# Query projections by halves of the sequence, the second half among the scores, and the first layer norm one sequence sooner

## What is computed

```python
x = x + _layernorm(attn(_layernorm(x)))     # below
x = x + _layernorm(ffn(_layernorm(x)))      # 8 experts, top 2, silu(x Wg) * (x Wu), Wd

q = relu(split(h @ Wq, 16)); k = relu(split(h @ Wk, 4)); v = split(h @ Wv, 4)
gk = log_sigmoid(split(h @ Wg1 @ Wg2 + bg2, 4)) / 16
# per head of 64: S_t = exp(g_t) * S_{t-1} + k_t (outer) v_t ; o_t = (q_t / 8) @ S_t
o = g_norm_weight * (o * rsqrt(mean(o * o) + 1e-6))
attn = o.reshape(b, t, 1024) @ Wo
```

## Time and profile before

| | |
|---|---|
| three runs | 1250.46, 1253.17, 1254.14 us; median 1253.17 |
| profiled execution | 1251.32 us, of which the span of the instructions is 1249.5 us |
| mean granted TensorE clock | 0.978 of full speed |
| busy in the span | PE 93%, DVE 62%, ACT 51%, POOL 44% |
| busy in 50 us of the first stage (265 to 315) | PE 47.3, DVE 38.7, ACT 28.6, POOL 27.3 us |
| chain that ended last | PE 69%, DVE 15%, issue 7%, ACT 4%, DMA 3% |

### The profile page before, as it was taken

The page is one execution under the profiler, slowest core; times in us unless marked ns, Lnnn a source line. Parts: engine busy times, 40 slices in busy tenths (PEclk is TensorE's granted clock), DMA queues, the critical chain, the costliest instruction groups (busy, mean ns, idle before and its releaser), DMA issues.

```text
span 1249.5 us, 29218 instructions
## 1 busy us (share of the span) xinstructions
PE 1158.4 (93%) x8910; PEld 942.3 (75%) x8910; DVE 769.4 (62%) x2380; ACT 640.8 (51%) x1653; POOL 556.0 (44%) x686
## 2 busy tenths in 40 slices
PE   8999999999999999999999999579999999999895
PEld 4867867768668678677686686569999989998762
DVE  5677777777777777777777876723333333333327
ACT  3655656547546556465475473334444444443336
POOL 2245464564654654645646544423333333333326
PEclk9999999999999999999999999879999999999998
DMA  7001010010110110100101101334111111111534
GB/s 277 10 27 31 13 43 19 24 34 17 34 34 11 40 32 11 42 17 25 39 12 34 34 4 35 139 89 133 47 49 49 47 49 46 49 49 44 177 124 176
DMA packets 59676, 67.50 MB, mean 54 GB/s; under 512 B 6896, under 2 KB 49664, under 8 KB 59264
## 3 DMA queue, kind: packets, MB, share of 16 engines
q1 hardware_dynamic: 48720, 41.10, 10.5%
q0 software_dynamic: 8448, 17.45, 4.2%
q10 hardware_dynamic: 2480, 8.61, 2.1%
HBM read 37.98 MB, written 29.15 MB: 54 GB/s over the span
## 4 chain that ended last, share of the span: by engine, by line
PE 69%; DVE 15%; issue 7%; ACT 4%; DMA 3%; DVEq 1%; POOL 1%; ACTq 0%; SPq 0%; POOLq 0%
PE pO L764 9%; PE pO L597 9%; PE pO L602 7%; PE pA L581 6%; PE pW L630 5%; PE pA L755 4%; PE pA L756 4%; PE pJ L755 4%; PE pJ L756 4%; PE pT L613 3%; DVE S_raw L1130 2%; DVE qT L1116 2%; PE pJ L630 2%; PE pJ L515 2%; DVE ss L1160 2%
## 5 line engine op out<-in xcount | busy, mean ns | idle before, releaser
L1630 POOL DMA_INDIRECT expert_out<-y,tail x136 | 130.5, 960 | 262.0 <-ACT y L1023 238.5
L874 ACT ACTIVATE sq<-pO 128x512 f32<-128x512 f32 x128 | 75.9, 593 | 211.7 <-PE pO L597 160.5
L597 PE MATMUL pO<-vJ,aT 128*128 128x128 f32 x1024 | 144.5, 285 | 14.4 <-DVE aT L1153 14.4
L597 PEld LDWEIGHTS pO<-vJ,aT 128*128 128x128 f32 x1024 | 128.7, 196 | 37.0 <-issue 34.1
L1542 POOL DMA_INDIRECT expert_rows<-x1n,rowi x120 | 120.5, 1004 | 50.0 <-issue 31.7
L1160 DVE TENSOR_REDUCE ss<-sq 128x8 f32<-128x512 f32 x128 | 87.1, 680 | 80.1 <-ACT sq L874 78.4
L764 PE MATMUL pO<-wdown_sb,vJ 128*128 128x128 f32 x1088 | 133.3, 276 | 0.0
L764 PEld LDWEIGHTS pO<-wdown_sb,vJ 128*128 128x128 f32 x1088 | 127.4, 193 | 0.0
L1408 DVE TENSOR_TENSOR vJ<-pA,kJ 128x256 f32<-128x256 f32 x136 | 57.5, 425 | 107.8 <-ACT kJ L1012 107.2
L602 PE MATMUL pO<-S_mid,qT 128*128 128x128 f32 x896 | 118.3, 275 | 0.0
L602 PEld LDWEIGHTS pO<-S_mid,qT 128*128 128x128 f32 x896 | 109.0, 192 | 0.0
(11 more groups left out here) (234 smaller groups left out, 2374.0 us busy)
## 6 DMA issues: line engine op xcount, KB each, us to landing
xt<-expert_rows SPq DMA_DIRECT2D x69, 130.0 KB
xa<-x SPq DMA_DIRECT2D x16, 256.0 KB, 2.8
xr<-x SPq DMA_DIRECT2D x16, 256.0 KB
after_attention<-x SPq DMA_DIRECT2D x16, 256.0 KB
arena<-after_attention ACTq DMA_DIRECT2D x8, 512.0 KB
expert_rows<-zeros SPq DMA_DIRECT2D x8, 390.0 KB
expert_out<-y,tail POOLq DMA_INDIRECT x136
wgate_sb<-wgate SPq DMA_DIRECT2D x1, 2048.0 KB, 9.4
```

Source lines behind the costliest of these rows:

```text
L597: last = mm(o[:, g, h, :, :], aT[:, c % 2, h, g * P:(g + 1) * P], vJ[:, c, h, :], start=(h == 0 and g == 0), stop=(c == 0), skip_group_che ...
L1630: g.indirect_dma_start(out=ys_dram, in_=y[:, k, :], in_offset=None, out_offset=bass.IndirectOffsetOnAxis(ap=tail[:, k, 1:2].bitcast(U32), ...
```

## The change

The eight query products are made for the first 256 tokens at the end of a turn as before, two products of 256 columns in one bank, and for the last 256 tokens as four pairs inside `chunks`: one before the first scores, one after them, one behind the second scores and one behind `outputs(i, 1)`. `scores(i, 0)` waits for the first four reads, `scores(i, 4)` for all eight. `query` on DVE reads a pair, and its last four are in `chunks`. In a bank the two products are interleaved in blocks of 64 columns (n r c), so that DVE reads and writes runs of 128; `grow` is kept twice over (ACT writes 1024 columns per pair instead of 512), in the place of the two gate buffers behind the others, and `on` moves to another place of the same arena.

The norm of sequence i + 2 begins in turn i: statistics at chunk 3 on DVE, rstd at chunk 3 on ACT, `norm_apply` on POOL between the first gate sum and the first gate difference. Router statistics move from chunk 0 to 1, `router_rstd` from 1 to 2 (ahead of `norm_T`), router transposes from 2 to 3. The last tile's `merged_apply` moves behind the first two masks, its residual on POOL behind `mids`. The query decays of pair 1 are made right after its key decays. The loops of ACT, DVE and POOL leave one turn more outside, for the last one has no norm ahead.

```diff
-            def project_queries(j, turns=range(PAIRS * R)):
-                for b in turns:
-                    if b < 2:
-                        pe.wait_ge(v_ready, j * 8 + 4 * b + 4)
-                    elif b < 4:
-                        pe.wait_ge(k_ready, j * 2 + b - 1)
+            def project_queries(j, half, turns=range(PAIRS * R // 2)):
+                for n in turns:
+                    if half == 0 and n < 2:
+                        pe.wait_ge(v_ready, j * 8 + 4 * n + 4)
+                    elif half == 0:
+                        pe.wait_ge(k_ready, j * 2 + n - 1)
                     else:
-                        pe.wait_ge(q_ready, j * 8 + b - 3)
-                    mm(four[b % 4][:], wq_sb[:, b // R, b % R, :], xnT[:],
-                       start=True, stop=True).then_inc(q_psum, 1)
+                        pe.wait_ge(q_ready, j * 8 + n + 3)
+                    for u in range(2):
+                        b = 2 * n + u
+                        last = mm(query_bank(n, half).rearrange("p (n r c) -> p r n c", r=2, c=C)[:, u, :, :], wq_sb[:, b // R, b % R, :],
+                                  xnT[:, half * (L // 2):(half + 1) * (L // 2)], start=True, stop=True)
+                    last.then_inc(q_psum, 1)
...
                 if c >= 2:
                     pe.wait_ge(a_ready, i * NC + c)
-                else:
+                if c == 0:
+                    pe.wait_ge(q_ready, i * 8 + 4)
+                elif c == 4:
                     pe.wait_ge(q_ready, i * 8 + 8)
...
+                project_queries(i, 1, range(0, 1))
                 scores(i, 0)
+                project_queries(i, 1, range(1, 2))
                 for c in range(NC):
                     outputs(i, c)
+                    if c == 1:
+                        project_queries(i, 1, range(3, 4))
                     if more and c == 2:
                         norm_transposes(i + 1, routed)
                     if c % 2 == 0 and c + 2 < NC:
                         scores(i, c + 2)
+                    if c == 0:
+                        project_queries(i, 1, range(2, 3))
                     if c in (3, 5, 7):
                         merge_heads(i, (c - 3) // 2, more)
                     if c > 0:
                         out_transposes(i, c - 1)
+                    if routed and c == (3 if more else 2):
+                        router_transposes(i - 1, i - 1, x1n)
                     if more and c in (2, 3):
                         gate_logits(i + 1, c - 2)
-                    if routed and c == 2:
-                        router_transposes(i - 1, i - 1, x1n)
...
             def query_decays(j, p):
-                a(grow[:, p, :], rel[:, p, :], ACT.Exp, scale=-1.0 / GATE_NORMALIZER).then_inc(decay_ready, 1)
+                a(grow[:, p, :, :, :], wide(rel[:, p, :].rearrange("p (n c) -> p n c", c=C).unsqueeze(2), P, NC, 2, C),
+                  ACT.Exp, scale=-1.0 / GATE_NORMALIZER).then_inc(decay_ready, 1)
...
-                    if more and c == 0:
+                    if more and at_start(i) and c == 0:
                         norm_rstd(i + 1)
-                    if routed and c == 1:
+                    if ahead and c == 3:
+                        norm_rstd(i + 2)
+                    if routed and c == (2 if more else 1):
                         router_rstd(i - 1, i - 1)
                     if more and c == 2:
                         norm_T(i + 1)
...
                     if more and c == 7:
-                        key_decays(i + 1, 1)
+                        decays(i + 1, 1)
...
-            def query(j, b):
+            def query(j, n, half):
                 dve.wait_ge(decay_ready, j * 4 + 4)
-                dve.wait_ge(q_psum, j * 8 + b + 1)
+                dve.wait_ge(q_psum, j * 8 + 4 * half + n + 1)
...
                     state(j, 0)
                     state(j, 1)
-                    merged_apply(merging, NT - 1)
-                for b in range(PAIRS * R):
-                    query(j, b)
...
+                    query(j, 0, 0)
+                    state(j, 2)
+                    query(j, 1, 0)
+                    query(j, 2, 0)
+                    state(j, 3)
+                    query(j, 3, 0)
...
+                for c in range(4, NC - 1):
+                    state(j, c)
...
                 mask(i, 0)
                 mask(i, 1)
-                if more:
+                if routed:
+                    merged_apply(i - 1, NT - 1)
+                query(i, 0, 1)
+                query(i, 1, 1)
+                if more and at_start(i):
                     norm_stats(i + 1)
                 for c in range(NC):
+                    if ahead and c == 3:
+                        norm_stats(i + 2)
                     head_norm(i, c, not more)
-                    if routed and c == 0:
+                    if c < 2:
+                        query(i, 2 + c, 1)
+                    if routed and c == (1 if more else 0):
                         router_stats(i - 1)
...
-                    if c == 1 and merging is not None:
-                        residual(merging, NT - 1)
...
-            def turn(i, routed, more):
-                if more:
+            def turn(i, routed, more, ahead):
+                if routed:
+                    residual(i - 1, NT - 1)
+                else:
                     norm_apply(i + 1)
...
                     gate_sum(i + 1, 0)
+                if ahead:
+                    norm_apply(i + 2)
+                if more:
                     gate_relative(i + 1, 0)
```

More of the change, by code:

```diff
@@ L128, in gate_view @@
             return flat[:, n * PAIRS * L:(n + 1) * PAIRS * L].rearrange("p (a l) -> p a l", a=PAIRS)
-        absz, relz, run, rel, grow, shrink = (gate_view(n) for n in range(6))
+        absz, relz, run, rel, shrink = (gate_view(n) for n in range(5))
+        grow = flat[:, 6 * PAIRS * L:8 * PAIRS * L].rearrange("p (a n r c) -> p a n r c", a=PAIRS, r=2, c=C)
         step_log = sb("step_log", [P, PAIRS, NC])
@@ L228, in build, with query_bank @@
         merge_bank = [pW[:, 0:HID], pJ[0][:, 0:HID], pW[:, 0:HID], pW[:, 0:HID]]
+        def query_bank(n, half):
+            return four[n][:] if half == 0 else four[2 + n % 2][:]
         def gate_bank(j, p):
@@ L700, in _ @@
             pe.wait_ge(q_in, 16)
-            project_queries(0, range(0, 1))
+            project_queries(0, 0, range(0, 1))
             key_transposes(0)
-            project_queries(0, range(1, 2))
+            project_queries(0, 0, range(1, 2))
             state_updates(0)
-            project_queries(0, range(2, PAIRS * R))
+            project_queries(0, 0, range(2, 4))
             pe.wait_ge(rest_in, 16 * len(REST_W))
@@ L716, in turn @@
                 state_updates(i + 1)
[L717 removed]
+                project_queries(i + 1, 0)
             turn(0, False)
@@ L932, in chunks @@
                     if more and c == 7:
-                        query_decays(i + 1, 1)
                         steps_of(i + 1)
@@ L974, in _, with turn @@
             act.wait_ge(rest_in, 16 * len(REST_W))
-            def turn(i, routed):
-                chunks(i, True, routed)
+            def turn(i, routed, ahead=True):
+                chunks(i, True, routed, ahead)
                 out_T(i, NC - 1)
@@ L982, in _ @@
             turn(0, False)
-            with act.Fori(1, S - 1) as i:
+            with act.Fori(1, S - 2) as i:
                 act.preload_act_table_set(LOG_EXP)
@@ L986, in _ @@
             act.preload_act_table_set(LOG_EXP)
-            chunks(S - 1, False, True)
+            turn(S - 2, True, False)
+            chunks(S - 1, False, True, False)
             router_T(S - 1, HALVES[0])
@@ L1139, in queries_and_states @@
                     state(j, 1)
-                    merged_apply(merging, NT - 1)
-                for b in range(PAIRS * R):
-                    query(j, b)
[L1143 to L1148, removed]
+                    query(j, 0, 0)
[5 more added lines that the diff above has]
+                else:
+                    for n in range(4):
+                        query(j, n, 0)
+                        state(j, n)
+                for c in range(4, NC - 1):
+                    state(j, c)
             def mask(i, c):
@@ L1360, in _ @@
             turn(0, False)
-            with dve.Fori(1, S - 1) as i:
+            with dve.Fori(1, S - 2) as i:
                 turn(i, True)
-            chunks(S - 1, False, True)
+            turn(S - 2, True, False)
+            chunks(S - 1, False, True, False)
             choose(S - 1, S - 1, HALVES[0])
@@ L1491, in router_norm, with mids @@
                                     ALU.subtract, ALU.mult).then_inc(x1n_ready, 1)
-            def mids(j, merging=None, after={}):
+            def mids(j, after={}):
                 pool.wait_ge(step_ready, j + 1)
@@ L1600, in turn, with turn_and_mids @@
                         scatter(1, n)
-            turn(0, False, True)
-            mids(1, 0)
```

(13 more changed lines are left out.)

14 lines of the change are left out of this document (9 added, 5 removed).

## The result

The changed kernel takes 1236.9 us (median of four runs, 1234.9 to 1240.0), the kernel before 1253.7 in the same comparison: a ratio of 0.987, 95% interval 0.985 to 0.989. Of the forecast's 21.5 us, 16.8 came, and 1236.9 lies just inside the upper end of the forecast of 1224 to 1237. The profiled execution took 1237.6 us, of which the span is 1234.5.

The account below looks back on a forecast made before the run. PE, busy 93% of the span, bounds the kernel, so only its waits or slow running can be won. Turns 9.8, turn 0 1.4, last turn 2.3 and clock 8.0 make 21.5 us: 1231 forecast, range 1224 to 1237 (wider 1214 to 1244).

Parts of the forecast that it names:

- the walk: One turn followed step by step on PE, DVE and ACT with durations from the profile: turn 0.70 us shorter.
- the pair of gaps: PE's waits before a turn's first scores and first outputs, 2.28 us; three short waits, 0.66 in all, should replace them.
- rival (2): DVE's stretch denser than counted: waits of 0.5 more a turn stay, or clock still falls; 1238 to 1246, chance 0.20.
- The gate logits' wait: New PE wait in chunk 2 for xnT, behind the router's statistics and rstd: 0.91 us lost per turn.
- the sum: Turns 1 to 14 9.8 us, turn 0 1.4, last turn 2.3, clock 8.0; together 21.5.
- Rival (1): The wait at the gate logits is hidden: 12.7 us more, 1218; chance 0.17.
- The clock: Five turns' falls of the granted clock behind the pair of gaps vanish, 1.6 us each, 8.0 in all.
- Turn 0: First turn, without router: scores start at 29.2 instead of 30.34 with two pairs still to come; gain 1.4 us.
- The last turn: No norm_T there: first half gives 1.6 us, PE's 0.81 wait for router rows mostly goes; gain 2.3.
- The other edits: Decays, norm a sequence sooner and moved residual lie under cover; norm_apply 3.13 us on POOL, from 335.2 to 338.3.
- rival (4): Query products slowed by writes in blocks of 64 columns; at twice their 0.86 us the kernel takes 1340; chance 0.03.
- rival (5): Late load of xa stops DVE in chunk 3, slower from 1.5 us a turn; with late decays, chance 0.07.

Follow-up runs that it names:

- the shifted kernel: The changed kernel with three empty instructions more on ACT and three on DVE ahead of their first turns; 1229.67 us, ratio 0.981 to before.

## Why the prediction was right, and where it was off

**The bound and the walk held.** Scores and sixth pair came within 0.01 us of the walk. Where signals are on time (the shifted kernel, its turn moved by 41.62 us) `outputs` came at 360.69 where the walk had 360.72, the router's statistics at 368.88 (walk 368.91), and `outputs(4)` at 377.64 (walk 377.80). The three short waits at the start of a turn replaced the pair of gaps. One remark made under rival (2) did not hold, that DVE has under 0.9 us free in this stretch: in the shifted kernel it stands idle 1.23 us in one wait alone. That costs nothing here, and it is why the statistics of the norm fit in at their old place.

**The gate logits' wait was mis-sized.** The step has 0.91 us per turn; in the run with `norm_T` first it proved to be 0.69, and 0.10 for the slower products behind it, so 0.79. The statistics stood where the walk had them, but from their start to that of the logits it took 2.50 us (373.42 to 375.92), not 2.71: two short instructions on ACT took 0.44 instead of 0.56, the copy 0.58 instead of 0.62, and PE followed 0.05 behind it, not 0.13. Without the late signals the turn is 0.88 shorter than 48.46, where the sum has 0.70. Rival (1), that the wait is hidden, did not happen. Where the signals are on time the whole gain is 23.2 us by the medians (1252.83 to 1229.67), against the sum's 21.5.

**The late signal stood in no step.** The walk lets DVE's mask start when DVE is free, at 364.01 by this turn's clock, and it started at 364.41. Of the 0.88 a turn this took back 0.43, in 13 turns 5.6 us: 12.7 for the turns 1 to 14 became 7.0, and the sum had 9.8. It is rival (2) in its price (waits of 0.5 a turn that stay) but not in its reason: DVE was not denser than counted, it stood still.

**The clock** was sized rightly inside the turns. All five falls in the turns are gone, at 1.57 us each 7.9 of the 8.0 counted, and the kernel before with filled gaps shows it by itself. The single wait at the gate logits led to none; but it is 0.53 us long and not the 0.91 of the forecast, so that no run here tests a single gap of that size. Slices below full clock remain at the start, which the second profiled execution of this kernel doesn't have, and from 782.6 to 786.0 us, in the hand-over to the experts, where the kernel before is still at full clock. The last tile's product by Wo, in before and then in after:

```profile
796.94 2.05 PE L630 MATMUL pW<-wo_sb,oT 128*128 128x128 f32 x16
```

```profile
782.39 3.63 PE L639 MATMUL pW<-wo_sb,oT 128*128 128x128 f32 x16
```

This fall costs 1.5 us, and no step of the forecast has it. Six of the eleven profiled executions with the split queries have it, so it doesn't come with the change as such; why some have it stays open.

**Turn 0 was over-valued**: 1.4 in the sum, 0.6 between the marks. The walk of a later turn was applied to it, but in turn 0 `queries_and_states` has another order: behind the last read four states come, not three, and the last of them starts only after DVE has stood idle 0.56 us for the one before it. The mask follows at 31.54, so PE's wait for it stayed as long as in a turn of before. DVE and then PE in turn 0 after:

```profile
31.15 0.47 DVE L1151 SCALAR_TENSOR_TENSOR S_raw<-S_raw,step,pO 128x64 f32<-128x64 f32 x2 [0.56 <-DVE S_raw L1151]
...
32.28 1.16 PE L606 MATMUL pO<-vJ,aT 128*128 128x128 f32 x8 [0.94 <-DVE aT L1177]
```

**The last turn** gave a little less than was counted. The sum has 2.3, and 1.6 for the fifth fall, 3.9 together. The last tile's product by Wo starts 44.70 us behind the last mark before and 41.34 after, so 3.4 came, and 3.7 where the signals are on time. The 0.81 that PE waited for router rows is gone. That 3.8 came in all behind the last mark is luck of this execution: the fall in the hand-over took 1.5 back, and the experts and the final norm, which the change doesn't touch, happened to take 2.0 less. They differ by 2.7 us between the two profiled executions of the kernel with ACT's and DVE's programs moved.

**The other edits** cost PE nothing. The blocks of 64: rival (4) fell, and with it, for this pattern, the rule of the Trainium skill that it rests on. The decays with 1024 columns took 1.04 us each, between the bounds of 0.6 and 1.2. `xa` landed in 3.0 us (2.8 before), and DVE waits for it once, 4.2 us at the start (4.5 before), and never in the turns, so rival (5) fell. `norm_apply` took 4.09 us where 3.13 was counted, from 381.24 to 385.33; that is 1 us of the cover of 1.6 that the step named.

Between the profiled spans lie 15.0 us, and between the medians 16.8. The start of the kernel and its last two stages, which moved by 2.7 and by 2.0 here, are each seen to vary by more than a microsecond from execution to execution of one kernel, so the difference of the two figures asks for no cause of its own.

## What to carry to other kernels

Walk the turn engine by engine before an edit: with durations from rows it placed every start of an undisturbed turn to 0.2 us, and it named the new wait, which one swapped pair on ACT then turned into 0.79 us a turn and the fastest kernel of the study. Don't blame a part of a change for half a microsecond per turn before an edit that moves the program but not the work has been timed beside it. Here 6 us seemed to be the price of the norm's new place and were not. Where the clock falls behind a gap, fill the gap in the old kernel first: it shows in one experiment what of a gain is the clock's.

## What the runs showed of the hardware

**A semaphore's signal may depend on where the program lies.** The signal of packed 64 x 64 score products came 0.42 us behind the start of the last one, or 0.90 to 1.02 for the first two groups of a turn, in a given program always in the same turns and groups; three empty instructions ahead of the loops, on PE or on ACT and DVE, removed it. The products themselves started on time, and in the turns compared the signals of PE's other products came on time too. Why is open.

**A tile on POOL takes 0.98 us longer while a scan runs on DVE.** POOL's four tiles of `norm_apply` took 4.09 us here, 3.14 at the old place. One of the four grows from 0.79 to 1.77, while DVE's scan (L1103) runs:

```profile
381.24 4.09 POOL L1497 TENSOR_SCALAR xn<-xa,mv,rstd 128x128 f32<-128x128 f32 x4
...
381.95 1.21 DVE L1103 TENSOR_TENSOR_SCAN arena<-in_chunk,arena 128x512 f32<-128x512 f32 x1
```

The times (min/median/max in ns) of all tiles, in the changed kernel and then in the one with the norm at its old place, where no tile meets the scan:

```profile
L1497 POOL TENSOR_SCALAR xn<-xa,mv,rstd x60: 788/792/1772, 36.2 to 672.5; 128x128 f32<-128x128 f32 x60
```

```profile
L1493 POOL TENSOR_SCALAR xn<-xa,mv,rstd x60: 783/788/812, 36.1 to 702.1; 128x128 f32<-128x128 f32 x60
```

One tile grows in each of the 14 turns that have this step.

The Trainium skill (SBUF — State Buffer, section "Who interferes with whom") says that DVE's second pair of ports is GpSimd's own, that the one excludes the other, and that a DVE instruction with two inputs in SBUF meets it when GpSimd reads SBUF. The scan reads two operands from SBUF, and the trace agrees with it: the tile grew by 0.98 us, which is most of the scan's 1.21.
